# A cross-attention and FFN kernel on one core: weight parts of the second layer spread over three engines, a product behind the scores, another bank for a bias row, and one projection unit moved

## What is computed

```python
x = x + _L0_xattn_ref(_layernorm(x), ctx, mask, bias, ln_w, w_q, w_k, w_v, w_out)   # 32 heads of 128, softmax over 128 keys, output projection
x = x + _L0_ffn_ref(_layernorm(x), W_base, b_base, lora_A, lora_B, router_W, router_b, prior, active)  # base product + 4 routed low-rank experts
x = x + _L1_xattn_ref(_layernorm(x), ctx, Wq, bq, Wk, bk)   # one head of 512; Q = x Wq' + bq, K = ctx Wk' + bk
x = x + _L1_ffn_ref(_layernorm(x), qweight, scale, zero, bias)  # 6-bit weights, unpacked, one product
```

## Time and profile before

| | us |
|---|---|
| median of 3 runs | 967.88 |
| the profiled execution | 970.49 |
| its span, first to last instruction | 968.7 |
| TensorE busy | 943.7 (97%) |
| VectorE busy | 636.8 (66%) |
| ScalarE busy | 407.9 (42%) |
| GpSimd busy | 516.7 (53%) |
| mean granted TensorE clock | 0.990 |

### The profile page before, as it was taken

One profiled execution on the slowest core, in us unless ns is written; L12 is line 12 of the kernel. 1 busy time (PEld: TensorE's weight loads), 2 busy tenths in 40 slices (PEclk: granted clock), 3 DMA queues, 4 the chain that ended last, 5 costly groups with the idle time before them and its releaser, 6 DMA issues.

```text
span 968.7 us, 16920 instructions
## 1 busy us (share of the span) xinstructions
PE 943.7 (97%) x5501; PEld 819.2 (85%) x5501; DVE 636.8 (66%) x1162; ACT 407.9 (42%) x1141; POOL 516.7 (53%) x579
## 2 busy tenths in 40 slices
PE   8999999999999999999999999999999997999996
PEld 7888888888889888988888888888888885777774
DVE  5665765555856685667666766676756678467885
ACT  5654425334343434443443343434334334234553
POOL 3450734476656655675557565756674632032567
PEclk9999999999999999999999999999999997999999
DMA  9224437663667356745683667365736563300001
GB/s 328 101 79 144 141 121 284 199 224 131 250 229 272 131 220 229 277 149 219 222 284 128 243 209 273 117 259 190 280 123 247 193 217 132 118 3 1 33 30 59
DMA packets 61146, 171.70 MB, mean 177 GB/s; under 512 B 6039, under 2 KB 8219, under 8 KB 60844
## 3 DMA queue, kind: packets, MB, share of 16 engines
q1 hardware_dynamic: 61100, 171.11, 50.0%
HBM read 159.56 MB, written 11.53 MB: 177 GB/s over the span
## 4 chain that ended last, share of the span: by engine, by line
PE 87%; DVE 7%; ACT 2%; issue 2%; POOL 1%; DMA 1%; POOLq 0%; SPq 0%; ACTq 0%; DVEq 0%
PE ps_o L347 6%; PE ps_q L347 6%; PE ps_q L349 6%; PE ps_q L348 6%; PE ps_o L349 6%; PE ps_o L348 6%; PE ps_k L347 5%; PE ps_t L2103 5%; PE ps_k L348 5%; PE ps_k L349 5%; PE ps_s L2076 5%; PE ps_v L347 5%; PE ps_v L349 5%; PE ps_v L348 5%; PE ps_t L2093 3%
## 5 line engine op out<-in xcount | busy, mean ns | idle before, releaser
L761 ACT ACTIVATE scores<-scores,neg_max 128x128 f32<-128x128 f32 x256 | 99.8, 391 | 234.9 <-DVE neg_max L1529 234.9
L1416 DVE TENSOR_TENSOR acc<-ps_o,acc 128x512 f32<-128x512 f32 x128 | 87.8, 686 | 64.1 <-PE ps_o L349 64.1
L347 PE MATMUL ps_o<-wo_hi,att_hi 128*128 128x512 f32 x256 | 107.1, 419 | 8.1 <-DVE att_lo L1404 7.4
L349 PE MATMUL ps_o<-wo_hi,att_lo 128*128 128x512 f32 x256 | 101.1, 395 | 0.0
L348 PE MATMUL ps_o<-wo_lo,att_hi 128*128 128x512 f32 x256 | 100.9, 394 | 0.0
L767 ACT COPY probs_t<-ps_t 128x512 f32<-128x512 f32 x64 | 37.6, 588 | 141.8 <-PE ps_t L2093 141.8
L1064 POOL TENSOR_TENSOR shift<-bias_sb,mask_sb 128x512 f32<-128x512 f32 x64 | 84.2, 1315 | 5.6 <-DVE scores L1525 5.6
L1404 DVE TENSOR_TENSOR att_lo<-ps_t,att_hi 128x512 fp32r<-128x512 f32 x64 | 44.2, 691 | 58.3 <-ACT att_hi L754 58.3
L1105 POOL TENSOR_TENSOR wq_lo<-raw_q,wq_hi 128x256 fp32r<-128x256 f32 x65 | 48.5, 746 | 59.9 <-ACT wq_hi L593 59.9
L347 PE MATMUL ps_v<-wv_hi,ct_hi 128*128 128x256 f32 x264 | 75.0, 284 | 0.3 <-POOL wv_lo L1085 0.2
L349 PE MATMUL ps_v<-wv_hi,ct_lo 128*128 128x256 f32 x264 | 74.7, 283 | 0.0
(11 more groups left out here) (375 smaller groups left out, 2774.1 us busy)
## 6 DMA issues: line engine op xcount, KB each, us to landing
ring_hi<-scratch_x_t SPq DMA_DIRECT2D x39, 512.0 KB, 4.1
ring_lo<-scratch_x_t SPq DMA_DIRECT2D x39, 512.0 KB, 4.9
ring_hi<-scratch_c_t SPq DMA_DIRECT2D x39, 512.0 KB, 4.1
ring_lo<-scratch_c_t SPq DMA_DIRECT2D x39, 512.0 KB, 5.4
raw_o<-in_w_o SPq DMA_DIRECT2D x16, 512.0 KB, 4.8
raw_q<-in_w_q SPq DMA_DIRECT2D x15, 512.0 KB, 6.4
raw_k<-in_w_k SPq DMA_DIRECT2D x15, 512.0 KB, 7.2
xt_hi<-scratch_x_t SPq DMA_DIRECT2D x13, 512.0 KB, 7.4
```

What stands on the lines that cost most here:

```text
L347: pe.matmul(dst, hi_l, hi_r, start=first, stop=False)
L349: return pe.matmul(dst, lo_l, hi_r, start=False, stop=last)
L761: e = act.activation(probs[n][:, m, :], scores[n][:, m, :], ACT.Exp, bias=neg_max[:, n, m:m + 1], accum_out=row_sum[:, n, m:m + 1])
L1416: dve.tensor_tensor(acc[:, b, :], ps_o[:], acc[:, b, :], ALU.add).then_inc(o_added, 1)
```

## The change

Five things are changed.

1. wk1: ScalarE casts the first two of the four parts before it copies out the probabilities of step 60, the other two after the cast of wo. The four low parts are made by GpSimd (after `rest_o` in step 60), no longer by VectorE. They count on another semaphore.
2. wq1: VectorE makes the four low parts at three places, two before the second `add_output` of step 61, one after it, and the last after `attention_rest` of step 61. In step 62 the first block of the weight product comes right behind the scores, and each output part one block later.
3. The bias row is spread into bank ps_q2 and waits for three of the four `mm_rest`; the small low-rank products wait for `select`, no longer for ScalarE's copy of the row.
4. In c = 0 of turns 2 to 7 TensorE makes q_p3 before the first v_p5, so before the transposes, no longer behind the values.
5. The small instructions of `act_chain` and the bias product move from behind step 7 to behind steps 2, 3 and 4; in step 8 GpSimd makes wo_lo before wv_lo.

```diff
--- before.py
+++ after.py
@@ -293,6 +293,7 @@
 
         w1_in = [sem("wk1_in"), sem("wq1_in0"), sem("wq1_in1")]
         w1_hi_s, w1_lo_s = sem("w1_hi_s"), sem("w1_lo_s")
+        wk1_lo_s = mask_done
         vec_in, bqk_s, vec_acc, vec_mm, vec_out = (
             sem(n) for n in ("vec_in", "bqk_s", "vec_acc", "vec_mm", "vec_out"))
         mm_done, mm_hi_s, mm_out = sem("mm_done"), sem("mm_hi_s"), sem("mm_out")
@@ -868,13 +869,19 @@
 
             attention_high(STEPS - 5)
             exponentials(STEPS - 4, 0)
-            pt_evac(STEPS - 4)
-            split_o(GROUPS - 1)
             act.wait_ge(w1_in[0], 16)
             act.wait_ge(q_done, 7 * GROUPS - 10)
             act.wait_ge(k_done, 7 * GROUPS - 10)
-            for c in range(NC):
+
+            def wk1_high_part(c):
                 act.copy(wk1_hi[:, c, :], wk1_raw[:, c, :]).then_inc(w1_hi_s, 1)
+
+            wk1_high_part(0)
+            wk1_high_part(1)
+            pt_evac(STEPS - 4)
+            split_o(GROUPS - 1)
+            wk1_high_part(2)
+            wk1_high_part(3)
             attention_high(STEPS - 4)
             exponentials(STEPS - 3, 1)
             act.wait_ge(q_done, 7 * GROUPS - 9)
@@ -893,7 +900,8 @@
             def mm_high(m):
                 act.wait_ge(mm_done, m + 1)
                 if m == 0:
-                    act.wait_ge(w1_lo_s, 2 * NC)
+                    act.wait_ge(wk1_lo_s, NC + 1)
+                    act.wait_ge(w1_lo_s, NC)
                     act.wait_ge(vec_mm, 1)
                 act.copy(mm_hi[:, m, :], m_banks[m][:]).then_inc(mm_hi_s, 1)
 
@@ -903,7 +911,7 @@
             for m in range(NC):
                 mm_high(m)
             act.wait_ge(kb_mm, 1)
-            act.copy(kb_row[:], ps_v[:]).then_inc(kb_s, 1)
+            act.copy(kb_row[:], ps_q2[:]).then_inc(kb_s, 1)
             act.wait_ge(lr_mm, 1)
             act.activation(logit_bias[:, 0, :], ps_v[:, 148:152], ACT.Ln, bias=prior_eps[:, 0:1]).then_inc(lbias, 1)
             exponentials(STEPS - 1, 1)
@@ -1222,10 +1230,15 @@
                     low_v(i + 1, 2, 0, v_even[1][:])
                 if c % 4 == 0 and more:
                     low_first(G)
+                if c % 4 == 0:
+                    rest_o(g)
                 if first:
                     rest_v(PLAIN)
-                if c % 4 == 0:
-                    rest_o(g)
+                if last and c == 4:
+                    for m in range(NC):
+                        pool.wait_ge(w1_hi_s, m + 1)
+                        pool.tensor_tensor(wk1_lo[:, m, :], wk1_raw[:, m, :], wk1_hi[:, m, :].bitcast(F32),
+                                           ALU.subtract).then_inc(wk1_lo_s, 1)
                 if c == 1 and own:
                     low_v(i, 6, 0, v_even[1][:])
                 if c == 5 and coming:
@@ -1589,6 +1602,11 @@
                     block_sub(wide[0], wide[0], wide[2])
                 if s > 0:
                     add_output(s - 1, (s - 1) % LOOP_STEPS, (1,))
+
+            def wq1_rest(m):
+                dve.wait_ge(w1_hi_s, NC + m + 1)
+                dve.tensor_tensor(wq1_lo[:, m, :], wq1_raw[m], wq1_hi[:, m, :].bitcast(F32),
+                                  ALU.subtract).then_inc(w1_lo_s, 1)
 
             def step(i, c):
                 s = LOOP_STEPS * i + c
@@ -1663,6 +1681,8 @@
                     v_c21(i, 1)
                 if last and c == 5:
                     k_c12(g)
+                    wq1_rest(0)
+                    wq1_rest(1)
                 if c == 5 and coming:
                     v_c11(i + 1, 1)
                 if c % 4 == 0 and summed:
@@ -1679,51 +1699,55 @@
                 if c == 7 and coming:
                     v_u3(i + 1, 1)
                 add_output(s - 1, (c - 1) % LOOP_STEPS, (1,))
-                if last and c == 4:
-                    for m in range(NC):
-                        dve.wait_ge(w1_hi_s, m + 1)
-                        dve.tensor_tensor(wk1_lo[:, m, :], wk1_raw[:, m, :], wk1_hi[:, m, :].bitcast(F32),
-                                          ALU.subtract).then_inc(w1_lo_s, 1)
                 if last and c == 5:
-                    for m in range(NC):
-                        dve.wait_ge(w1_hi_s, NC + m + 1)
-                        dve.tensor_tensor(wq1_lo[:, m, :], wq1_raw[m], wq1_hi[:, m, :].bitcast(F32),
-                                          ALU.subtract).then_inc(w1_lo_s, 1)
+                    wq1_rest(2)
 
             def step_drain(s, c):
                 softmax_front(s, c % 2)
                 softmax_back(s, c % 2)
                 add_output(s - 1, c - 1)
 
+            def target_experts():
...
+            def target_rows():
...
+            def target_copies():
...
+            def bias_product():
...
             for s in range(FIRST):
                 step_first(s)
-
-            dve.wait_ge(act_in, 48)
-            dve.wait_ge(iota_s, 2)
-            dve.tensor_copy(act_f[:, 0, :], act_i[:]).then_inc(act_chain, 1)
...
-            dve.wait_ge(bqk_s, 1)
-            dve.tensor_reduce(bqk_sum[:], bqk_mul[:], AX_X, ALU.add).then_inc(bqk_s, 1)
+                if s == 2:
+                    target_experts()
+                if s == 3:
+                    target_rows()
+                if s == 4:
+                    target_copies()
+                    bias_product()
 
             for c in range(LOOP_STEPS):
                 step(1, c)
@@ -1772,6 +1796,7 @@
                                   ALU.bitwise_and).then_inc(unp, 1)
 
             attention_rest(STEPS - 3)
+            wq1_rest(3)
             softmax_front(STEPS - 2, 0)
             add_output(STEPS - 3, 5, (0,))
             softmax_back(STEPS - 2, 0)
@@ -2343,6 +2368,7 @@
                 if c % 4 == 3:
                     k_p4(G)
                 if c == 0 and own:
+                    q_p3(g)
                     v_p5(i, 0)
                 if c == 1:
                     if own:
@@ -2375,7 +2401,8 @@
                 else:
                     step_values(s, c, v_count(i, (1, 2, 11, 12, 13, 14, 14, 14)[c]))
                 if c % 4 == 0 and not (last and c == 4):
-                    q_p3(g)
+                    if c == 4 or not own:
+                        q_p3(g)
                     if c == 0 and own:
                         v_p5(i, 1)
                     if c == 4:
@@ -2408,13 +2435,13 @@
             def product_m(m):
 
                 if m == 0:
-                    pe.wait_ge(w1_lo_s, NC)
+                    pe.wait_ge(wk1_lo_s, NC + 1)
                     pe.wait_ge(q_comb, 7 * (GROUPS - PLAIN))
                     pe.wait_ge(k_comb, 7 * (GROUPS - PLAIN))
                 cols = slice(m * P, (m + 1) * P)
                 for c in range(NC):
                     if m == 0:
-                        pe.wait_ge(w1_lo_s, NC + c + 1)
+                        pe.wait_ge(w1_lo_s, c + 1)
                     last = three(pe, m_banks[m][:], wk1_hi[:, c, cols], wk1_lo[:, c, cols], wq1_hi[:, c, :],
                                  wq1_lo[:, c, :], c == 0, c == NC - 1)
                 last.then_inc(mm_done, 1)
@@ -2444,16 +2471,16 @@
 
             def spread_kb():
 
-                pe.wait_ge(sel_s, 1)
-                pe.matmul(ps_v[:], ones[:], w_rows[:, 1, :], start=True, stop=True).then_inc(kb_mm, 1)
+                pe.wait_ge(mm_out, 3)
+                pe.matmul(ps_q2[:], ones[:], w_rows[:, 1, :], start=True, stop=True).then_inc(kb_mm, 1)
 
             s = STEPS - 2
             wait_projections(GROUPS - 1, 6)
             step_scores(s, 6)
+            product_m(0)
             output(s - 1, 5, None, (0,))
-            product_m(0)
+            product_m(1)
             output(s - 1, 5, None, (1,))
-            product_m(1)
             step_transpose(s, 6)
             product_m(2)
             step_values(s, 6, v_count(TURNS - 1, 14))
@@ -2474,7 +2501,7 @@
             output(s - 1, 6, None, (0,))
             spread_kb()
 
-            pe.wait_ge(kb_s, 1)
+            pe.wait_ge(sel_s, 1)
             pe.wait_ge(rbc_s, 2)
             pe.wait_ge(lora_in, 48)
             for c in range(NC):
```

More of the change, by code:

```diff
@@ new lines, in target_rows @@
+            def target_rows():
+                dve.wait_ge(act_chain, 6)
+                for j in range(ACTIVE):
+                    dve.scalar_tensor_tensor(targets[:, j * RANK:(j + 1) * RANK],
+                                             targets[:, STACK + j:STACK + j + 1].broadcast_to([1, RANK]),
+                                             float(RANK), iota_rf[:], ALU.mult, ALU.add).then_inc(act_chain, 1)
+            def target_copies():
+                dve.wait_ge(act_chain, 10)
+                for k in range(1, 3):
+                    dve.tensor_copy(targets[:, k * RR:(k + 1) * RR], targets[:, 0:RR]).then_inc(act_chain, 1)
```

35 lines of the change are left out of this document (16 added, 19 removed).

## The result

The changed kernel takes 957.41 us (median of 4 runs, 957.01 to 958.23) against 967.69 (4 runs, 967.22 to 968.49): ratio 0.9894, 95% interval 0.9877 to 0.9911, 10.3 us less. The forecast was 956.5 and the range 952.5 to 960.8.

A forecast was written before the change was run, and what follows sets the result against it. TensorE, busy 943.7 of 968.7 us, was taken to bound the kernel, so its waits were targeted. Savings of 3.9 + 1.7 + 5.0 + 0.8 = 11.4 us from the 967.88 median gave 956.5 us, range 952.5 to 960.8.

The forecast's parts named there:

- Part 1: c = 0 of turns 2 to 7: q_p3 ahead of the transposes hides the wait for probabilities, -3.9 us.
- The rival that the move does nothing: In the loop, q_p3 waits itself or the transposes wait as before: 960.4 us, chance 0.08.
- Part 2: First steps: moved small instructions and wo_lo first remove TensorE's pauses in steps 8 and 9, -1.7 us.
- Part 3: Last turn: wk1, wq1 and product-order changes cut pauses and half-clock loss from 10.8 to 5.8 us, -5.0 us.
- First pause 0.7: Last turn, before the output of step 60: TensorE waits 0.7 us, until wo_lo ends.
- Second pause 2.9: Before step 61's transposes: TensorE waits 2.9 us for probabilities, with row_fac and scaling delayed by GpSimd.
- The rival that GpSimd does not hold up VectorE: Step 61: probabilities ready at 808.9, pause 1.3 us, clock stays up; about 953.5 us, chance 0.15.
- the rival that most VectorE instructions of steps 61 and 62 are held: Last turn gives little: three more 1.2 us waits for GpSimd cost 3.6 us; about 960 us, chance 0.13.
- Clock 1.6: Last turn, behind the pause before step 61's transposes: 3.3 us at half speed, charged as 1.6 us.
- Part 4: Bias row in ps_q2: TensorE's 0.68 us wait for ScalarE's copy goes, 0.84 with the modelled end, -0.8 us.
- the third half-clock stretch: Small low-rank products behind the bias row: 6.5 us at half clock, expected unchanged; vanishing would free about 1.3 us.
- the first rival: Step 61: GpSimd does not hold up VectorE; about 953.5 us, entered in the range as 953, chance 0.15.

The follow-up runs named there:

- the last variant: Changed kernel with two wk1 low parts ahead of wo_lo, GpSimd's shifts held until step 61's scaled probabilities, and att_hi before ScalarE's last two wk1 casts: 954.53 us.
- the held variants: Changed kernel with GpSimd work held until step 61's probabilities are scaled: all four wk1 low parts, 957.97 us; or the shifts, with two low parts early, 954.67 us.
- part 3 alone: Kernel before with only the wk1, wq1 and product-order changes: 962.77 us, ratio 0.9944.
- the first group: Runs on one chip of four kernels, each with one part of the change, beside the unaltered kernel before: 968.58 us for the latter (20 runs).
- Parts 2 and 4 alone: Two kernels on the kernel before: small instructions earlier and wo_lo before wv_lo, 967.48 us; bias row in ps_q2, 965.27 us.
- The four parts alone: Kernel before with one part each: q_p3 earlier 965.98 us, first-steps changes 967.48, wk1/wq1/product order 962.77, bias row in ps_q2 965.27.

## Why the prediction was right, and where it was not

**Part 1** (-3.9): 4.0 in the traces of the pair, 3.3 in its own trace, 3.2 with an interval of 2.1 to 4.2 in the runs. The wait went away wholly, as said, and att_lo in c = 1 was in time. The rival that the move does nothing fell.

**Part 2** (-1.7): 1.6 in both traces, 1.4 in the runs.

**Part 3** (-5.0): 5.5 in the pair of traces, 5.4 in the runs. By its own terms:
- First pause 0.7, ended by wo_lo: shown as 0.54, which is 0.70 with the 0.16 that the prediction adds for the modelled end. That wo_lo ends it, the last variant shows.
- Second pause 2.9: 2.47, or 2.63 in the same count. Row_fac was held 0.36 us (0.5 expected), the scaling 1.03 (1.2 expected). That GpSimd is the cause is shown by the held variants, with 0.16 and 0.69 us. The rival that GpSimd does not hold up VectorE fell with them; the rival that most VectorE instructions of steps 61 and 62 are held did too, as behind the scaling only wq1's first two low parts (2.42 us for two, 1.28 in other variants) were.
- The 0.55 for an addition ahead of the output and for wq1's last part did not come: TensorE has no wait above 0.04 us there. This is about the 0.5 us by which part 3 brought more than its 5.0.
- Clock 1.6: 1.60 where the stretch is there, nothing where it is not.
- The order of the product, said to bring nothing by itself but to cover att_lo: 1.23 us of wait and 1.5 us of time come back without it.

The rule of the Trainium skill that was weighed there (page "SBUF — State Buffer", section "Who interferes with whom") gave 957.3 when both instructions were taken at the worst phase. The trace agrees with its exclusion and not with the worst phase: the scaling lost 1.03 us of a wk_lo's 1.25. The same section names `tensor_scalar` among the instructions that can take the shared ports; neg_max, a TENSOR_SCALAR, with 1.18 us in the last variant agrees, and it was left out of that variant's expectation.

**Part 4** (-0.8) is the term that was wrong. The wait of 0.68 us went as said. "I leave the third half-clock stretch as it is" failed: it is 3.4 us long in eight of the nine profiles with part 4 and absent in one, and 6.8 in four of the five without part 4 and absent in one. The small products, to which the text put the stretch down, were the same in all. Steps 62 to 63 are 2.4 us shorter, so the clock gives 1.6 on top of the wait. The text had priced the case in which the stretch vanishes at 1.3, as the softmax then holds the next output. That wait, 1.2 us, did appear in both executions without the stretch, for an addition to acc that stands behind the softmax on VectorE, and part 3 alone gained 1.9 there (23.11 us against 24.98). The size was thus known roughly, and the wrong case was chosen. Why the clock recovers earlier without the wait was not measured apart from the rest of part 4.

**From the profiled execution to the median.** The terms sum to 11.4, the pair of profiles differs by 13.0, the medians by 10.3 in one comparison and 11.8 in another. The profiled execution of before was among its slowest (970.49): it had 17.0 us at half clock, and the executions of before differ in this. Of the 20 runs of the first group, the seven with a mean granted clock of 0.990 have a mean time of 969.4 us, the seven with 0.994 one of 968.0. Subtracting from the median a saving that was read from such an execution charges the change with clock that the median doesn't lose. Parts 2 and 4 alone show the same from another side: they leave steps 61 to 62 as they were, with the same wait of 2.0 us, and these took 14.4 us against 15.73, as the second stretch was absent. This error of up to 2.7 us (13.0 less 10.3) and the 1.6 missing in part 4 have opposite signs, so it is partly luck that the forecast lies 0.9 us from the result. In the range, the first rival enters with 953 where its own sum gives 953.5; nothing hangs on that.

The four parts alone bring 3.2 + 1.4 + 5.4 + 3.2 = 13.2 us, the whole 10.3 and 11.8, each with an interval of 1.0 to 1.6 either way. That a half-clock stretch can be saved only once would explain a sum that is too large, but within the intervals this stays open.

## What to carry to other kernels

Moving work from VectorE to GpSimd frees VectorE only for instructions that GpSimd's do not hold up (here att_lo took its 0.69 us beside wo_lo, the scaling 1.72 beside wk_lo): write down GpSimd's queue with its times and see which VectorE instructions of the critical chain fall beside it. Here leaving GpSimd idle for 1.7 us, with two low parts made early, was worth 1.3 us of trace over the changed kernel at the same clock. And before a saving is subtracted from a median, compare the clock of the profiled execution with that of the other runs.

## What was not expected of the hardware

The same kernel with the same pauses had its clock fall in one execution and not in another: changed kernel, pauses of 0.54 and 2.47 us with 3.4 us at 0.50 behind them, and 0.54 and 2.48 us with none. In the last steps the clock also fell without a wait of TensorE shown ahead of it: during the small low-rank products of the changed kernel TensorE is shown busy for the whole time at full clock (with ends that are modelled),

```profile
830.60:833.50 2.90, 2.90 (x21) 2.66 (x19) 0.00 (x0) 1.87 (x2) 0.00 (x0) 1.00 1.02 386
```

and at 834 us the clock is 0.50, in the large products behind them. With a wait of 0.7 us ahead of the small products the stretch was twice as long in four profiles and absent in one. And instructions of 128x4 elements can cost VectorE as much as large ones: neg_max 1.18 us in place of 0.17 beside GpSimd. The trace of before had shown this already, with a neg_max of 0.63 us at 810.12 beside a GpSimd shift.
